# A four-stage recurrence: p's step partly summed on TensorE, another order of the last stage, and longer loops

## The reference

```python
def _derivative(q, p, drive, coupling, bias):
    i_couple = jnp.tanh(q) @ coupling.T
    dq = q - q ** 3 / 3.0 - p + drive + i_couple + bias
    dp = EPSILON * (q + ALPHA - BETA * p)
    return (dq, dp)
def _rk4_step(q, p, drive, coupling, bias):
    dq1, dp1 = _derivative(q, p, drive, coupling, bias)
    dq2, dp2 = _derivative(q + 0.5*DT*dq1, p + 0.5*DT*dp1, drive, coupling, bias)
    dq3, dp3 = _derivative(q + 0.5*DT*dq2, p + 0.5*DT*dp2, drive, coupling, bias)
    dq4, dp4 = _derivative(q + DT*dq3, p + DT*dp3, drive, coupling, bias)
    q_next = q + DT/6 * (dq1 + 2*dq2 + 2*dq3 + dq4)
    p_next = p + DT/6 * (dp1 + 2*dp2 + 2*dp3 + dp4)
    return (jnp.clip(q_next, -CLAMP, CLAMP), jnp.clip(p_next, -CLAMP, CLAMP))
```

## Time and profile before

| | us |
|---|---|
| median of 3 runs | 5927.5 (5925.9 to 5928.78) |
| the profiled execution | 5931.63 |
| its span, first to last instruction | 5929.8 |
| PE busy | 4508.3 (76%) |
| DVE busy | 5526.4 (93%) |
| ACT busy | 2595.9 (44%) |

### The profile page before, as it was taken

The page is one execution under the profiler, slowest core; times in us unless marked ns, Lnnn a source line. Parts: engine busy times, 40 slices in busy tenths (PEclk is TensorE's granted clock), DMA queues, the critical chain, the costliest instruction groups (busy, mean ns, idle before and its releaser), DMA issues.

```text
span 5929.8 us, 592455 instructions
## 1 busy us (share of the span) xinstructions
PE 4508.3 (76%) x263627; PEld 3814.4 (64%) x263627; DVE 5526.4 (93%) x31560; ACT 2595.9 (44%) x12040; POOL 5.6 (0%) x16
## 2 busy tenths in 40 slices
PE   7887777777777777777777777777777777777777
PEld 3446666666666666666666666666666666666666
DVE  6569999999999999999999999999999999999999
ACT  3334444444444444444444444444444444444444
POOL 0000000000000000000000000000000000000000
PEclk9999999999999999999999999999999999999999
DMA  5100000000000000000000000000000000000000
GB/s 211 45 16 0 0 7 0 7 0 7 0 0 7 0 7 0 7 0 0 7 0 7 0 7 0 0 7 0 7 0 7 0 0 7 0 7 0 7 0 7
DMA packets 11597, 57.06 MB, mean 10 GB/s; under 512 B 2616, under 2 KB 2616, under 8 KB 8512
## 3 DMA queue, kind: packets, MB, share of 16 engines
q1 hardware_dynamic: 11056, 55.84, 2.4%
q10 hardware_dynamic: 528, 1.05, 0.0%
HBM read 40.11 MB, written 16.78 MB: 10 GB/s over the span
## 4 chain that ended last, share of the span: by engine, by line
DVE 44%; PE 34%; issue 11%; ACT 10%; DMA 1%; DVEq 0%; SPq 0%; ACTq 0%
PE ps L619 29%; DVE xb L661 23%; DVE turned_sums L811 10%; ACT xb L437 7%; DVE tanh_parts L661 4%; ACT tanh_parts L443 3%; DVE xb L936 2%; DVE xb L834 2%; PE ps L508 1%; DVE xb L932 1%; DVE xb L927 1%; PE ps L563 1%; PE ps L526 1%; PE ps L552 1%; PE ps L542 1%
## 5 line engine op out<-in xcount | busy, mean ns | idle before, releaser
L619 PE MATMUL ps<-coup,tanh_parts 128*16 128x96 f16 (+1 forms) x262272 | 4159.4, 219 | 1345.7 <-DVE tanh_parts L661 680.6
L619 PEld LDWEIGHTS ps<-coup,tanh_parts 128*16 128x16 f16 x262272 | 3653.2, 89 | 1852.4 <-issue 863.9
L437 ACT ACTIVATE xb<-xb 128x24 f32<-128x24 f32 (+1 forms) x4098 | 940.7, 230 | 2968.7 <-DVE xb L661 2958.5
L661 DVE SCALAR_TENSOR_TENSOR xb<-xb 128x64 f32<-128x64 f32 x11267 | 2198.2, 214 | 17.7 <-issue 0.2
L661 DVE SCALAR_TENSOR_TENSOR xb<-turned_sums,step_scale,xb 128x64 f32<-128x64 f32 (+2 forms) x6145 | 1601.2, 261 | 16.2
L811 DVE STREAM_TRANSPOSE turned_sums<-ps 128x96 f32<-128x96 f32 (+1 forms) x4096 | 1284.2, 314 | 142.2 <-PE ps L619 67.3
L661 DVE SCALAR_TENSOR_TENSOR tanh_parts<-xb,tanh_parts 128x24 f16<-128x24 f32 (+1 forms) x4098 | 712.8, 174 | 49.9
L443 ACT ACTIVATE tanh_parts<-xb 128x24 f16<-128x24 f32 (+1 forms) x2050 | 470.9, 230 | 64.5
L481 ACT ACTIVATE xb<-xb 128x64 f32<-128x64 f32 x2048 | 498.8, 244 | 0.0
L834 DVE SCALAR_TENSOR_TENSOR xb<-xb 128x64 f32<-128x64 f32 x2049 | 445.6, 217 | 0.1
L455 ACT ACTIVATE tanh_parts<-xb 128x24 f16<-128x24 f32 (+1 forms) x2048 | 357.4, 221 | 32.1
(11 more groups left out here) (68 smaller groups left out, 792.7 us busy)
## 6 DMA issues: line engine op xcount, KB each, us to landing
xb<-in_x SPq DMA_DIRECT2D x8, 2048.0 KB, 7.9
drive<-in_x_pt SPq DMA_DIRECT2D x8, 2048.0 KB, 24.6
out_pt<-drive SPq DMA_DIRECT2D x16, 1024.0 KB, 4.5
drive<-in_coupling_t SPq DMA_DIRECT2D x8, 512.0 KB, 11.5
mask_v<-in_cond SPq DMA_DIRECT2D x8, 132.0 KB
probs<-in_wo ACTq DMA_DIRECT2D x1, 1024.0 KB, 5.5
w_qkv<-in_wq SPq DMA_DIRECT2D x1, 64.0 KB, 3.8
w_qkv<-in_wk SPq DMA_DIRECT2D x1, 64.0 KB, 5.2
```

Source lines behind the costliest of these rows:

```text
L437: nc.scalar.activation(cols(tanh_sb, CHUNKS[j]), cols(q, CHUNKS[j]), ACT.Tanh)\
L619: last = nc.tensor.matmul(product(s, j)[SQ * g:SQ * g + ROWS, :], tanh_parts[:, s % 2, k, :], coup[:, k, part, g, n0:n1, :].rearrange("p c ...
L661: return V.scalar_tensor_tensor(out=out, in0=a, scalar=factor, in1=c, op0=ALU.mult, op1=op1)
```

## The change

It has three parts.

1. **Loops.** `PE_STAGES` becomes 4 (`STAGES`) and `UNROLLED` 8. DVE's loop body grows from 151 to 613 instructions of the built program, ACT's from 66 to 258, and PE's from 264 to 530, where each of its matmuls stands for a weight load and a matmul.
2. **The order of the last stage and of the gaps.** In stage 3 `clip_p` now stands in the gap before `q_of` of chunk 0 and `drive_less_p` in the gap after it. After `rest_of` of chunk 1 the order is `z_of_first`, `cubic_of`, `with_first_part`, `g0_of`, `base_of`. `drive_step_of` and `look_ahead` (both read `drive`) are in stage 1.
3. **p's step.** PE sums four terms in PSUM (`p_sum`, bank 4) with four fp32 matrices `p_shares`, each the unit matrix times a number: g0 and q0 after the product of stage 0, q1 after that of stage 1, q2 after that of stage 2. DVE adds the sum to p (`p_without_last`) and the last term (`p_next`) in stage 2. Four axpys go, one new one comes that reads PSUM, so there are two where there were five.

```diff
-PE_STAGES = 2
-UNROLLED = 2
+PE_STAGES = STAGES
+UNROLLED = 8
...
+            def share_of_p(k, state_of):
+                return nc.tensor.matmul(p_sum, p_shares[k], state_of[:, :], start=(k == 0),
+                                        stop=(k == len(P_SHARES) - 1), skip_group_check=True)
...
+                    if s == 0:
+
+                        pe.wait_ge(base_ready, now)
+                        share_of_p(0, g0)
+                        share_of_p(1, q_st[0])
+                    if s == 1:
+                        share_of_p(2, q_st[1])
+                    if s == 2:
+                        share_of_p(3, q_st[2]).then_inc(p_summed, STAGES)
...
-            def base_of(stage, made):
+            def base_of(stage, made, linear=None):
 
                 dve.wait_ge(cubic_ready, made)
+                if linear is not None:
+
+                    dve.wait_ge(zero_ready, linear)
...
                 if now is not None:
                     dve.wait_ge(drive_p_ready, now)
+                    dve.wait_ge(clipped, steps_until(now))
                 return axpy(z[:, :], drive_p[:, :], DT / 2, q_st[0][:, :])
...
+            def p_without_last(now):
+                dve.wait_ge(p_summed, now)
+                axpy(p_half[:, :], p_sum, DT / 6 * EPS, p_st[:, :]).then_inc(p_half_ready, STAGES)
+
+            def p_next(now):
+                dve.wait_ge(p_half_ready, now)
+                axpy(p_raw[:, :], q_st[3][:, :], DT / 6 * EPS, p_half[:, :]).then_inc(p_raw_ready, STAGES)
...
                 if s == 1:
-                    p_sum_g0()
+                    drive_step_of((now + 2) * (COLS // STAGES))
                 if s == 2:
                     q_sum_r2()
                 if s == 3:
-                    look_ahead((now + STAGES) * (COLS // STAGES))
+                    clip_p(now)
...
-                if s == 2:
-                    p_sum_q2()
                 if s == 3:
-                    p_next()
+                    drive_less_p(now)
...
                     q_sum_r1()
-                    drive_step_of((now + 2) * (COLS // STAGES))
+                    look_ahead((now + 2 + STAGES) * (COLS // STAGES))
...
                 if s == 3:
-                    clip_p()
                     clip_q(made)
-                    drive_less_p(now)
...
-                    p_sum_r1()
+                    less_q_of()
                     base_of(2, made)
-                    less_q_of()
                 if s == 2:
                     forecast_first(made)
+                    p_without_last(now)
                     dve.wait_ge(z_rest_ready, now)
                     with_first_part(3, z_first_part, z_rest)
                     cubic_of(3, made)
-                    p_sum_q3()
+                    p_next(now)
                     base_of(3, made)
                 if s == 3:
                     z_of_first(now).then_inc(z_ready, STAGES)
+                    cubic_of(0, made)
+                    dve.wait_ge(z_ready, now)
+                    with_first_part(0, z_first_part, z).then_inc(zero_ready, STAGES)
                     g0_of()
-                    dve.wait_ge(z_ready, now)
-                    with_first_part(0, z_first_part, z)
-                    cubic_of(0, made)
-                    base_of(0, made)
+                    base_of(0, made, now)
```

More of the change, by code:

```diff
@@ L71 @@
 Q_KEPT = 1 - THIRD - Q_STEP[0] * Q_STEP[1] - (CURVE * OFFSET - STEP[3] - THIRD)
-P_ALL = 1 + P_SUM[2]
+P_SHARES = [P_SUM[0], -1 - P_SUM[1] - P_SUM[2], P_SUM[1], P_SUM[2]]
 CHUNKS = [(0, 3), (3, 8)]
@@ L192, in build @@
         q_sum = [state() for k in range(3)]
-        p_sum = [state() for k in range(4)]
+        p_half = state()
+        p_shares = []
+        for k in range(len(P_SHARES)):
+            first = next(states)
+            next(states)
+            p_shares.append(xb[:, :, :].rearrange("p c n -> p (c n)")[:, first:first + P])
         z_rest = state()
@@ L265, in build @@
         p_ready = sem("p_ready")
+        p_shares_ready = sem("p_shares_ready")
+        p_summed = sem("p_summed")
+        p_half_ready = sem("p_half_ready")
+        p_raw_ready = sem("p_raw_ready")
+        zero_ready = sem("zero_ready")
         q_share_ready = sem("q_share_ready")
@@ L274, in cols @@
             return t[:, B * blocks[0]:B * blocks[1]]
+        p_sum = ps[:, 2 * NCH, 0:COLS]
         def by_block(t, blocks):
@@ L626, in products @@
                 return last
+            def share_of_p(k, state_of):
+                return nc.tensor.matmul(p_sum, p_shares[k], state_of[:, :], start=(k == 0),
+                                        stop=(k == len(P_SHARES) - 1), skip_group_check=True)
+            pe.wait_ge(p_shares_ready, 1)
             pe.wait_ge(start_ready, NCH + 1)
@@ L781, in _ @@
             attend(B - 1, False)
+            for k, share in enumerate(P_SHARES):
+                last = V.tensor_scalar(p_shares[k], ident[:, :], share, None, ALU.mult)
+            last.then_inc(p_shares_ready, 1)
             V.memset(ps[:, 0:2 * NCH, :].rearrange("p a n -> p (a n)"), 0.0)
@@ L908, in g0_of, with clip_p @@
                 axpy(g0[:, :], p_st[:, :], -BETA, q_st[0][:, :])
[L910 to L926, removed]
+            def p_without_last(now):
[4 more added lines that the diff above has]
+                axpy(p_raw[:, :], q_st[3][:, :], DT / 6 * EPS, p_half[:, :]).then_inc(p_raw_ready, STAGES)
+            def clip_p(now):
+                dve.wait_ge(p_raw_ready, now)
                 V.tensor_scalar(p_st[:, :], p_raw[:, :], -CLAMP - SHIFT, CLAMP - SHIFT, ALU.max, ALU.min)\
@@ L964, in _ @@
             dve.wait_ge(setup, 10)
+            g0_of()
             base_of(0, 1)
-            g0_of()
             def stage(s, now):
```

## The result

| | before | after |
|---|---|---|
| median | 5928.1 us (4 runs) | 6110.4 us (6107.5 to 6111.6, 4 runs) |
| ratio to before | | 1.0307 (95% interval 1.0289 to 1.0325) |
| the profiled execution's span | 5929.8 us | 6108.2 us |
| PE / DVE / ACT busy | 76% / 93% / 44% | 86% / 88% / 42% |

A forecast was written before the change was run, and what follows sets the result against it. Bound: the chain through DVE, PE and ACT, not simply DVE. From 5931.6: -51 + 12 - 72 + 10 + 15 = 5845.6; with code misses - 12 + 167 + 30 = 6030.6, less 4 is 6027 us; range 5825 to 6085.

The forecast's parts named there:

- The bound and the pace: One recurrence stage: a closed circle of product, transpose, new q, tanh, REST sets 2.62 to 2.64 us; stage 3 to 0 takes 2.74.
- The turns: DVE's loop: 254 turns at 0.20 us, 51 us, become 62 turns, 12 us at the same price; ACT's and PE's cost nothing.
- The store: DVE's 613-instruction body exceeds its instruction store: each of 62 turns waits 2.7 us for code, 167 us; chance 0.63.
- The sign of the packets: About 300 packets of 8 KB on q14 through the recurrence, and a DVE gap of 2 to 3 us every eighth step.
- Rival A: DVE's loop stays in the instruction store: 5842 us (5815 to 5880), faster by 1.4%; chance 0.31.
- B: DVE misses its code at turns, but cheaply: 1.6 us a turn spends the gain, 1.4 gives 5917 us; chance 0.05.
- D: PE misses its code too, at 512 turns: about 1500 us more, 7500 us; chance 0.02.
- The order of stage 3: Stage 3's end: 0.04 us from operations leaving before `rest_of`, 0.10 from `cubic_of` moving ahead; 72 us off, 10 back.
- "slack and 0.02": Stage 3's new register instruction and waits eat perhaps the slack and 0.02 us beyond a step, 10 us back.
- p's step: Four axpys removed from gaps save nothing; the new PSUM-reading operation ending stage 2 costs 0.03 us a step, 15 us (0 to 31).
- Rival C: PE's shares don't fit between the products: 0.15 to 0.2 us on each step, 77 to 102 us; chance 0.05.
- Borders inside the body: Four code-portion borders in DVE's body load each pass, a break of 0.24 us each, half hidden in waits: 30 us.

## Why the prediction was right or wrong

**The bound and the pace.** Right. 2.62 to 2.64 a stage is the circle through PE; with the block of stage 3 shortened it is 2.63 in all four.

**The turns.** Right. 254 turns at 0.20 became 62, and with four steps a body, where nothing is loaded, a turn still costs 0.20: 2.82 against 2.62.

**The store.** Right in direction and in the price of one load: 2.71 a turn against 2.7. Its three parts were right too. They were 0.9 until the packet, 0.51 for it and 1.55 from its end; behind the 62 turns they are 1.03, 0.43 and 1.37 from the branch on, as means. The sign of the packets was as named: q14 active through the recurrence, the gap at every eighth step. They are seven a turn where about five were expected, since the turn lies inside a portion and one more is loaded ahead. Rival A (it fits), B (a cheap miss) and D (PE misses too) are out. The store's size was left open; four portions, with one given away, fit the runs.

**The clock.** This is the step that failed: a term that the sum did not have. The prediction took DVE's wait as the only cost of a load, and so the product behind it as 2.02 us long. PE stands still for 2.90 us, behind 58 of 62 turns the granted clock falls to half, and the two stages behind the turn take 1.17 us more on average; 62 x 1.17 = 73 us, most of the 83 from 6027 to 6110. The prediction looked at the recurrence alone, where the trace of before has only idle of up to 0.84 us between products, with full clock. But the attention in the same trace shows what a longer pause does. Two of its groups of matmuls, behind pauses of 2.83 and 2.94 us, and the clock in the second:

```profile
81.27 1.92 PE L542 MATMUL ps<-probs_t,v_sb 128*32 128x512 f32 x16 [2.83 <-DVE drive L661]
...
127.70 3.57 PE L542 MATMUL ps<-probs_t,v_sb 128*32 128x512 f32 x16 [2.94 <-DVE drive L661]
```

```profile
127.83:131.24 3.41, 3.41 (x16) 0.50 0.53 213
```

All six pauses of 2.94 us there are followed by a half clock, and the same 16 matmuls take 3.2 to 3.6 us in place of 1.9; behind the one of 2.83, and one of 1.89, the clock stays full. The term could have been priced from these rows, at more than a microsecond a turn.

**The order of stage 3.** Half wrong. What left the stretch ahead of `rest_of` gave its 0.05. `cubic_of` ahead of `with_first_part` was to give 0.10 and gave nothing. Against the list of starts in the prediction, the trace has `z_of_first` at 0.18 behind `rest_of` where 0.13 stood (0.18 in the trace of before, too), `with_first_part` at 0.20 where 0.14 stood, and `base_of` at 0.19 where 0.14 stood; the "slack and 0.02" for the waits was too little. In all 72 - 10 = 62 us were forecast, and 31 measured.

**p's step.** Right that the four axpys in gaps saved nothing, since stages 0 to 1, 1 to 2 and 2 to 3 take 2.62, 2.64 and 2.64 as before. The new one in stage 2 cost 0, my lower bound, where I took 0.03; my upper one should have been 13.43 - 13.24 = 0.19, not 0.20, which changes nothing. The two shares of stage 0 last 0.66 us on PE, between my 0.5 and 0.79:

```profile
3016.57 0.66 PE L642 MATMUL ps<-xb 128*128 128x64 f32 x4
3017.41 2.01 PE L632 MATMUL ps<-coup,tanh_parts 128*16 128x96 f16 x128 [0.18 <-ACT tanh_parts L456]
```

They end before the next product, with 0.18 us idle left. Rival C is out.

**Borders inside the body.** 30 us were forecast, at 0.12 for each of four; 14 came. Of five borders two cost 0.11 each and the other three under 0.01.

**How near the rest came.** 6038, the measured time without the 73 us of the clock, is near the 6027 of the forecast in part by luck: stage 3 gave 31 us less than forecast, while p's step and the borders took 15 and 16 less, and about 9 lie in the first pass, the ends and the step from the profiled execution to the median.

## What to carry to other kernels

A longer loop body saves its turns only as long as the engine's instructions stay in its store; look for packets on an instruction queue in the steady state, and count the instructions of the body, waits and register work included, against what has been seen to stay. When one engine's stall makes TensorE stand, price not only the stall but the work behind it at half clock, and look for pauses of that length anywhere in the trace you have. Where a block of operations holds the pace, its starts have to be read with their waits: here another order of the same operations only moved the waits, and work moved ahead, out of the block, helped.

## What the runs showed of the hardware that had not been expected

- A DVE loop of 385 instructions was loaded anew at each turn and one of 309 was not; both would fit 32 KB (24.6 and 19.8 KB).
- A jump back to code that is gone took DVE 2.71 us over the usual distance, one to code that is there 0.20.
- TensorE's granted clock stayed full after all 127 pauses of 1.37 us. It fell to half after 126 of 127 pauses of 2.83 us, but only after 58 of 62, 60 of 83 and 65 of 100 of about 2.9 us in three other kernels. Then the same product took 3.2 us in place of 2.0.
